# A Flamingo-style stack on one core: the last attention in another order, and the last feed-forward's input normed and rounded inside it

## What is computed

```
x = x + tanh(g_xattn[3]) * attention(layernorm(x), ctx)
x = x + tanh(g_ffn[3]) * mx_ffn(layernorm(x))

attention: rmsnorm, 32 query heads and 8 key/value heads of 16 features, softmax(q k / 4) v, output matrix
mx_ffn:    gate = mx(x) @ mx4(w_gate).T;  up = mx(x) @ mx4(w_up).T          (512 -> 1376)
           y = mx(silu(gate) * up) @ mx4(w_down).T                           (1376 -> 512)
mx:        blocks of 32 features share a power of two; each element is rounded to a 6-bit float and clipped
mx4:       the same for weights, to a 4-bit float
```

## Time and profile before

| | |
|---|---|
| median of 3 runs | 1824.54 us (1823.87 to 1826.28) |
| the profiled execution's own time | 1822.57 us |
| its span in the profile | 1820.7 us |
| busy: PE, DVE, ACT, POOL | 1511.1, 1011.8, 358.7, 67.0 us |
| mean granted clock of PE | 0.885 of 2.4 GHz |
| attention stage, first transposed maxima to the last update of x | 1347.9 to 1633.3 us |
| feed-forward stage, first x transposed to the end | 1648.8 to 1820.7 us |

### The profile page before, as it was taken

One profiled execution on the slowest core, in us unless ns is written; L12 is line 12 of the kernel. 1 busy time (PEld: TensorE's weight loads), 2 busy tenths in 40 slices (PEclk: granted clock), 3 DMA queues, 4 the chain that ended last, 5 costly groups with the idle time before them and its releaser, 6 DMA issues. The chain is left out here.

```text
span 1820.7 us, 26629 instructions
## 1 busy us (share of the span) xinstructions
PE 1511.1 (83%) x8875; PEld 918.7 (50%) x8875; DVE 1011.8 (56%) x1644; ACT 358.7 (20%) x705; POOL 67.0 (4%) x92
## 2 busy tenths in 40 slices
PE   1799759999999867979999999987779899974554
PEld 0576623444444355657777777754364555521221
DVE  2666568887741173235666666653423423337886
ACT  0333321111131031011121121111013222211121
POOL 3000020000000000000000000001400000000000
PEclk9899859999999978989999999978878778776777
DMA  5000011111000080000000000003000000000000
GB/s 192 1 0 0 1 35 35 36 35 34 13 1 0 19 203 27 0 10 21 25 20 24 21 19 23 21 14 98 1 1 1 1 0 0 0 0 6 12 12 18
DMA packets 52310, 44.55 MB, mean 24 GB/s; under 512 B 38497, under 2 KB 38689, under 8 KB 51362
## 3 DMA queue, kind: packets, MB, share of 16 engines
q1 hardware_dynamic: 52258, 43.85, 8.0%
HBM read 41.74 MB, written 2.10 MB: 24 GB/s over the span
## 5 line engine op out<-in xcount | busy, mean ns | idle before, releaser
L924 DVE TENSOR_SCALAR f_side<-f_chunk 128x1536 f16<-128x1536 f32 x165 | 148.0, 953 | 45.7 <-PE f_sum L768 44.4
L768 PE MATMUL f_sum<-f_side,f_diag 128*128 128x512 f16 x495 | 121.7, 388 | 8.9 <-DVE f_side L924 7.3
L768 PEld LDWEIGHTS f_sum<-f_side,f_diag 128*128 128x128 f16 x495 | 47.7, 99 | 91.1 <-issue 43.4
L1565 PE MATMUL a_ps_b<-h_all,weights_a 128*128 (+1 forms) x768 | 92.0, 279 | 1.3 <-PEq L124 1.3
L1565 PEld LDWEIGHTS a_ps_b<-h_all,weights_a 128*128 128x128 f32 x768 | 89.0, 195 | 5.9 <-issue 5.9
L1653 PE MATMUL a_ps_y<-weights_a,a_o_t 128*128 128x512 f32 x192 | 89.2, 612 | 2.7 <-DVE a_v_ones L1785 2.0
L787 PE MATMUL f_gate<-h_all,f_w_t 128*128 128x512 f32 (+1 forms) x176 | 87.4, 597 | 0.0
L787 PE MATMUL f_up<-h_all,f_w_t 128*128 128x512 f32 (+1 forms) x176 | 79.6, 592 | 0.0
L2160 PEld LDWEIGHTS a_ps_a<-h_all,weights_a 128*128 128x128 f32 x512 | 72.7, 231 | 11.0 <-issue 11.0
L2160 PE MATMUL a_ps_a<-h_all,weights_a 128*128 (+1 forms) x512 | 75.5, 318 | 2.6 <-DVE a_sel L2396 2.6
L839 PE MATMUL f_sum<-weights_a 128*128 128x512 f32 (+1 forms) x176 | 75.7, 592 | 0.0
(11 more groups left out here) (316 smaller groups left out, 2776.6 us busy)
## 6 DMA issues: line engine op xcount, KB each, us to landing
f_chunk<-in_l_w SPq DMA_DIRECT2D x30, 256.0 KB, 3.0
weights_a<-in_l_wgu SPq DMA_DIRECT2D x16, 232.0 KB
weights_a<-in_l_wq SPq DMA_DIRECT2D x48, 64.0 KB, 2.4
weights_a<-in_l_wo SPq DMA_DIRECT2D x1, 3072.0 KB, 11.7
weights_a<-in_l_wd SPq DMA_DIRECT2D x16, 192.0 KB, 3.1
x_res<-in_x SPq DMA_DIRECT2D x1, 2048.0 KB, 8.2
ctx_nat<-in_ctx SPq DMA_DIRECT2D x1, 2048.0 KB, 13.3
ctx_tr<-in_ctx_tr SPq DMA_DIRECT2D x4, 512.0 KB, 13.4
```

Source lines behind the costliest of these rows:

```text
L768: mm = nc.tensor.matmul(psum[:, j, :], diag[:, k, :], side[:, k % RING, j * D:(j + 1) * D], start=(k == 0), stop=(k == LEVELS - 1), skip_g ...
L924: nc.vector.tensor_scalar(side[:, k % RING, :], wch[:, u, :], bounds[k], steps[k][0], ALU.is_le if k < ZERO else ALU.is_gt, ALU.mult).then ...
L1565: mm = nc.tensor.matmul(pb[:, u % 2, g * P:(g + 1) * P], wq_of(k, u, g), h_t[:, k, bass.ds(b * P, P)], start=(k == 0), stop=(k == KT - 1))
```

## The change

Stage 7, PE. `scores_t` takes two units at once: their first matmuls side by side, then the second, then the third. By the order of heads the two units of a pair read different groups of 32 rows and write different banks. There are four pairs a step in place of eight units. `keys_and_values` is split: only the keys stand ahead of the scores, the values behind unit 0. The first half of `weighted_values` moves into the step's middle, the second to its end, behind `maxima_as_rows`; `output(b - 1)` is cut into two halves that stand between score units 2 and 3 and behind 3. The four `weights_transposed` now lie between the queries, the keys and the third pair. ACT's order follows: `weights_stored(b, 0)` behind two exponentials, and the other three behind the queries' and keys' copies and behind six exponentials.

Stage 7, DVE and POOL. `updated(b - 1)` moves behind `maxima_spread(n)` and now finishes mean and variance of its batch (three instructions); POOL, idle until then, takes the power for each batch. `RoundedInput` norms and rounds batch b - 2: `begun` (norm and eight instructions) at the step's start, ahead of `q_lo` of the next batch, `ended` (two) behind `back`. The result goes into `weights_b`, over the first piece of step b - 2, which has been transposed by then. Batches 5 and 6 follow in the last step, batch 7 in stage 8.

Stage 8. `layernorm_all` and the rounding of x are gone but for batch 7, which DVE rounds first while PE begins with batch 0. PE waits for no rounding of x in the loop, and DVE's loop is products, update, hidden rounding.

The diff, cut to its core:

```diff
+class RoundedInput:
...
+    def meanvar(self, dve, b, count, x_updated):
+        nc, chip = self.chip.nc, self.chip
+        after(dve, *x_updated)
+        nc.vector.bn_stats(self.stats[:, :], chip.x_at(b)).then_inc(self.s_mv, 1)
+        after(dve, self.s_mv, count * 3 + 1)
+        nc.vector.bn_aggr(self.mv[:, :], self.stats[:, :]).then_inc(self.s_mv, 1)
+        after(dve, self.s_mv, count * 3 + 2)
+        nc.vector.tensor_tensor(chip.ln_mv[:, bass.ds(b, 1), :].rearrange("p a n -> p (a n)"), self.mv[:, :],
+                                self.eps[:, :], ALU.add).then_inc(self.s_mv, 1)
+
+    def rstd(self, pool, b, count):
+        chip = self.chip
+        after(pool, self.s_mv, count * 3 + 3)
+        chip.nc.gpsimd.tensor_tensor(chip.ln_rstd[:, bass.ds(b, 1)],
+                                     chip.ln_mv[:, bass.ds(b, 1), 1:2].rearrange("p a n -> p (a n)"),
+                                     chip.ln_mhalf[:, 0:1], ALU.pow).then_inc(self.s_rstd, 1)
+
+    def begun(self, dve, b, count, rstd_here=True):
+        chip, mx = self.chip, self.mx
+        if rstd_here:
+            after(dve, self.s_rstd, count + 1)
+        chip.nc.vector.tensor_scalar(self.h[:, :], chip.x_at(b), chip.ln_mv[:, bass.ds(b, 1), 0],
+                                     chip.ln_rstd[:, bass.ds(b, 1)], ALU.subtract, ALU.mult).then_inc(self.s_h, 1)
+        after(dve, self.s_h, count + 1)
+        mx.powers(dve, self.h[:, :], P, D)
+        mx.scales(dve, count, P, D, 3)
+        mx.magic(dve, count, P, D, 3)
+        mx.shift(dve, count, self.h[:, :], P, D, t1=self.h[:, :], t2=self.of(b))
+
+    def ended(self, dve, b, count):
+        self.mx.clip(dve, count, self.of(b), P, D, self.s_xq, t2=self.of(b))
...
+            @block.gpsimd
+            def _(pool):
+                rounded.constants(pool)
+                with pool.Fori(0, NB) as b:
+                    rounded.rstd(pool, b, b)
...
-                def scores_t(b, s, n):
-
-                    g = ORDER[n]
-                    c, r = g // RG, slice(32 * (g % RG), 32 * (g % RG) + 32)
-                    if n == 0:
+                def scores_t(b, s, pair):
+
+                    units = []
+                    for n in (2 * pair, 2 * pair + 1):
+                        g = ORDER[n]
+                        units.append((n, g // RG, slice(32 * (g % RG), 32 * (g % RG) + 32)))
+                    if pair == 0:
                         after(pe, s_nmb, b + 1)
-                    if n >= 2:
-                        after(pe, s_pt, b * KV3 + (n - 1))
-                    at = slice(c * QG * P, (c + 1) * QG * P)
-                    keys = k4[r, s, c * P:(c + 1) * P]
-                    nc.tensor.matmul(pst[:, n % 2, :], keys, qhi[r, s, at], start=True, stop=False,
-                                     skip_group_check=True)
-                    nc.tensor.matmul(pst[:, n % 2, :], keys, qlo[r, s, at], start=False, stop=False,
-                                     skip_group_check=True)
-                    nc.tensor.matmul(pst[:, n % 2, :], sel2[r, c, :], nmb[r, :, :].rearrange("p i t -> p (i t)"),
-                                     start=False, stop=True, skip_group_check=True).then_inc(s_st, 1)
+                    else:
+                        after(pe, s_pt, b * KV3 + 2 * pair)
+                    for part in (qhi, qlo):
+                        for n, c, r in units:
+                            nc.tensor.matmul(pst[:, n % 2, :], k4[r, s, c * P:(c + 1) * P],
+                                             part[r, s, c * QG * P:(c + 1) * QG * P], start=(part is qhi), stop=False,
+                                             skip_group_check=True)
+                    for n, c, r in units:
+                        nc.tensor.matmul(pst[:, n % 2, :], sel2[r, c, :], nmb[r, :, :].rearrange("p i t -> p (i t)"),
+                                         start=False, stop=True, skip_group_check=True).then_inc(s_st, 1)
...
                     scores_t(b, s, 0)
                     if not last:
                         queries(n, range(0, 4))
+                    weights_transposed(b, 0, first=not before)
                     scores_t(b, s, 1)
                     if not last:
                         queries(n, range(4, 8))
-                    scores_t(b, s, 2)
-                    if not last:
-                        keys_and_values(n)
-                    scores_t(b, s, 3)
-                    weights_transposed(b, 0, first=not before)
-                    scores_t(b, s, 4)
                     weights_transposed(b, 1)
                     if not last:
+                        keys(n)
+                    weights_transposed(b, 2)
+                    scores_t(b, s, 2)
+                    weights_transposed(b, 3)
+                    if not last:
                         scores(n, 1 - s, 0)
-                    scores_t(b, s, 5)
-                    weights_transposed(b, 2)
+                        values(n)
+                    weighted_values(b, s, 0)
                     if not last:
                         scores(n, 1 - s, 1)
-                    scores_t(b, s, 6)
-                    weights_transposed(b, 3)
-                    scores_t(b, s, 7)
+                    scores_t(b, s, 3)
                     if not last:
                         scores(n, 1 - s, 2)
                     if before:
-                        output(b - 1)
-                    weighted_values(b, s, 0)
-                    weighted_values(b, s, 1)
+                        output(b - 1, range(0, 2))
                     if not last:
                         scores(n, 1 - s, 3)
+                    if before:
+                        output(b - 1, range(2, 4))
+                    if not last:
                         maxima_as_rows(n)
+                    weighted_values(b, s, 1)
...
-                    row_stats(chip, dve, b, s_x, b + 2)
+                    rounded.meanvar(dve, b, b, (s_x, b + 2))
...
-                def step(b, s, before=True):
+                def step(b, s, before=True, rounds=True):
                     n = b + 1
+                    if rounds:
+                        rounded.begun(dve, b - 2, b - 2)
                     front(n, 1 - s)
-                    for unit in range(3):
+                    maxima(n, 0)
+                    values(n, 1 - s)
+                    for unit in range(1, 4):
                         maxima(n, unit)
+                    maxima_spread(n)
                     if before:
                         updated(b - 1)
-                    maxima(n, 3)
-                    maxima_spread(n)
                     back(b)
-
+                    if rounds:
+                        rounded.ended(dve, b - 2, b - 2)
+
+                dve.wait_ge(rounded.s_eps, 2)
                 front(0, 0)
-                for unit in range(4):
+                maxima(0, 0)
+                values(0, 0)
+                for unit in range(1, 4):
                     maxima(0, unit)
                 maxima_spread(0)
-                step(0, 0, before=False)
-                with dve.Fori(0, NB // 2 - 1) as pair:
-                    for u in range(2):
-                        step(pair * 2 + (u + 1), 1 - u)
+                step(0, 0, before=False, rounds=False)
+                step(1, 1, rounds=False)
+                with dve.Fori(1, NB // 2 - 1) as pair:
+                    for u in range(2):
+                        step(pair * 2 + u, u)
+                step(NB - 2, 0)
+                rounded.begun(dve, NB - 3, NB - 3)
                 updated(NB - 2)
                 back(NB - 1)
+                rounded.ended(dve, NB - 3, NB - 3)
+                rounded.begun(dve, NB - 2, NB - 2)
+                rounded.ended(dve, NB - 2, NB - 2)
                 updated(NB - 1)
...
-    layernorm_all(chip, "f3", transposed=False)
...
-                    after(pe, s_xq, b + 1)
...
-                with pe.Fori(0, NB - 1) as b:
+
+                def step(b):
                     x_transposed(b + 1)
                     gate_and_up(b + 1, 0)
                     gate_and_up(b + 1, 1)
                     hidden_transposed(b)
                     gate_and_up(b + 1, 2)
                     down(b)
+
+                with pe.Fori(0, NB - 2) as b:
+                    step(b)
+                pe.wait_ge(rounded.s_xq, 1)
+                step(NB - 2)
...
-                def both_ended(b, before=True):
...
-                    mh.powers(dve, hid[:, :], P, HF)
-                    if before:
-                        updated(b - 1)
-                    mx.shift(dve, b + 1, x_of(b + 1), P, D)
-                    mh.scales(dve, b, P, HF, 3)
-                    mx.clip(dve, b + 1, xq[:, :], P, D, s_xq)
-                    mh.magic(dve, b, P, HF, 3)
-                    mh.shift(dve, b, hid[:, :], P, HF)
-                    mh.clip(dve, b, hq[:, :], P, HF, s_hq)
...
-                x_begun(1)
-                both_ended(0, before=False)
-                with dve.Fori(0, NB - 2) as b:
```

(14 more changed lines are left out.)

95 lines of the change are left out of this document (58 added, 37 removed).

## The result

The changed kernel takes 1732.8 us (median of 4 runs, 1728.32 to 1734.24) against 1825.4 (1823.87 to 1827.19) before: a ratio of 0.949, 95% interval 0.947 to 0.951. Its profiled execution took 1732.03 us, its span is 1730.3; busy are PE 1442.4 us, DVE 1014.9, ACT 355.4, POOL 69.4, and the mean granted clock of PE is 0.911.

A forecast was written before the change was run, and what follows sets the result against it. PE, at a mean clock of 0.77, was taken to bound the attention, DVE the feed-forward. Savings of 71.6 + 0.9 + 9.3 + 1.4 = 83.2 us off 1822.57 gave 1739.4, forecast as 1740, range 1717 to 1784.

The forecast's parts named there:

- Its likeliest case: Whole kernel: 1722 to 1757 us, with pairs at 0.94, waits of 1 to 3.5 us, feed-forward period 19.2 to 20.5; chance 0.60.
- A step of the attention: Stage 7 on PE: 24.1 us of work and 2.1 of waits, 26.2 us a step; the attention 71.6 us less.
- The clock stays up: Attention on PE: small work cut up between full-size matmuls, so the step was taken at 2.4 GHz throughout.
- the fall at 1472: Old attention step: PE's clock falls in 9 us of small work only, from 1467.3 to 1476.4 us.
- The first rival: Attention: the clock still falls in each step, 29.8 to 33.4 us a step, kernel 1765 to 1787, say 1774; chance 0.20.
- DVE under it at no cost: Attention on DVE: rounding fits idle time before `q_lo`, with 3 us to spare; costs nothing, uncovered 6 to 7.5 us a step.
- The sign named for "wrong": Attention: one of the signs against the forecast, `q_lo` released by DVE itself instead of ACT's copy.
- The values off the path: Ahead of the attention's first transposed maxima: the values leave the path to score unit 0, 0.9 us less.
- POOL: Attention and seam: POOL's power of one column takes at most 1.64 us and has a whole step in the attention.
- The seam: Between the attention's last matmul and PE's start in the feed-forward: 9.3 us less, with DVE late by 1.6 us.
- The feed-forward: Stage 8: period stays 19.7 us, its chain starting at 1.2 GHz; first batch saves 4.4, last loses 3.0: 1.4 us less.
- The second rival: Feed-forward: PE keeps its clock, seven periods of 17.4 us, kernel 1724 us; chance 0.07.

The follow-up runs named there:

- the two halves of the change: Two runs against the kernel before: new attention order with stage 8 as before, 1746.4 us; rounding moved with PE's and ACT's old order, 1804.2 us.
- the next run: Changed kernel with late update, 20 extra matmuls a round, 40 before the last batch's hidden transposes, batch 6's last two rounding instructions behind the attention's last update: 1707.7 us.

## Why the prediction was right, and where not

The forecast was 1740, the measurement 1732.8. Its likeliest case was the one that came: the time lies in its 1722 to 1757.

- **A step of the attention.** 26.2 us forecast, 25.8 measured, at full clock; the pairs at 0.75 us right; waits of 1.2 us instead of 2.1. The first two steps were forecast as 53.2 and took 52.9, the last, to PE's last matmul, as 29.6 and took 27.3. The attention so gave 76.2 us for 71.6: this term was low by 4.6, of which 2.0 are the five steps and 2.3 the last.
- **The clock stays up.** Right in five steps of seven. The reason given, the small work cut up between full-size blocks, is not refuted, but shown only in part: serial pairs cost no clock, putting the output and the weighted values together none that can be told from chance, and both with the transpositions moved brought it down in five steps of six. And the working saw only the fall at 1472; the old step had another stretch of some 7 us at 1.2 GHz at its start, behind two waits, and this is gone with the change as well. Nor is the new order quite safe: in both runs with extra transposes, whose attention is the changed kernel's, two steps out of seven took 27.4 and 27.5 us at 0.94. There the fall came behind score unit 0, after 3.1 us of transpositions, a pair and that unit.
- **The first rival's page.** By the rule on transposes in the Trainium skill, "TensorE: Matmul & The Clock Gate", Part 4, the blocks of weight transposes would weigh like gaps. The runs speak against it: the changed attention has the four blocks and keeps its clock in five steps, and in the feed-forward 90 transposes kept it as well as 24 matmuls did.
- **DVE under it at no cost.** Right, shown by the two halves of the change. But the working was off: DVE works 18.3 us a step, not 20.5, but `begun` ends 13.9 us behind the spread maxima (1428.55 to 1442.42), not 12.5, PE is through the queries sooner, and the 3 us to spare are 0.3. The sign named for "wrong", `q_lo` released by DVE itself, did come; it was too strict a sign.
- **The values off the path, 0.9.** Keys to score unit 0 shrank by 0.8 us (3.91 to 3.08), but the first queries took 0.9 more, at a lower clock: nothing left.
- **POOL** took 0.55 us, under the bound of 1.64.
- **The seam.** From PE's last matmul 5.7 us, forecast 6.3; the late DVE cost 1.6, as worked out, and the run with the order alone shows just that difference. It gave 9.9 us for 9.3.
- **The feed-forward: the term that was mis-sized.** The chain at 1.2 GHz behind an idle PE is as forecast (idle for 7 to 8 us, transposes of 1.33, DVE idle 1.9 to 2.9 us before the update). But the periods are 18.5, 19.5 and 20.0 in turn, 19.2 in the mean, where 19.7 was taken and 19.2 was the lower end. The clock comes back at different places of `down`: the update stands 6.1, 7.0 and 7.5 us behind the rounding. Seven periods are 134.6 us, as much as the old six and the shorter last (134.9), so the 3.0 us forecast as lost were not. The first batch saved 5.1 for 4.4, and the end 0.4: 5.9 us for 1.4.
- **The total.** The span fell by 90.4 us for a forecast of 83.2. The attention was put 4.6 us too low, the feed-forward 4.5 and the seam 0.6; against them stand 0.7 of the values' 0.9 us, which did not come, and the 1.7 us ahead of the first queries. The three terms all erred in the same direction, and none by much.
- **The second rival,** 17.4 us at full clock, was about right as a price: 17.6 to 17.8 where extra work kept the clock. What the sum did not see is that the wait before the update, which it took as given, was a matter of where the update stands on DVE: 16 us.

## What to carry to other kernels

Read the granted clock beside PE's busy share: here, by the estimate above, some 8.5 of the 11.8 us that each step gave up were clock, with PE busy before and after. And where an in-order engine bounds a loop, look at what it waits for inside the loop before looking at its work: moving one instruction of 0.75 us five places down gave 16.1 us, as much as taking the norm and rounding of x out of the stage (15.3). Price hidden work by the slack at the point where it is consumed, not by the engine's idle time in the loop: DVE still idles 7.5 us a step, and 2.5 us more ahead of `q_lo` cost 2.2 and then the clock.

## What was not expected of the hardware

- Transposes kept PE's clock like matmuls of full size (90 of 0.058 us against 24 of 0.22 us: periods equal within 0.02 us).
- Whether the clock falls depends on more than the order: with 24 extra matmuls a round and PE idle for 1.7 to 3.0 us before the chain, it stayed at 2.4 GHz in three rounds (1.7, 2.7 and 3.0 us) and was back at 1.2 in four (2.8 us each), in the same loop. With 20 and the late update, at 1.7 to 2.5 us, it stayed in all seven; in the next run, with the same loop, the first round lost it at 2.5 us.
- Two units on 32 rows each take 0.75 us side by side on different rows and 1.39 one after the other on the same rows (the run changed the rows and the order of issue at once). The Trainium skill, "TensorE: Matmul & The Clock Gate", in its practical table, has small-K matmuls in distinct row groups run concurrently; the rows agree.
